# Attention of one batch woven with the projections of the next on TensorE, with 64-row score tiles and feed-forward weights streamed in pieces

## What is computed

```python
x = x + tanh(g_xattn) * attn(layernorm(x), ctx)       # ctx: 32 x 750 x 384
x = x + tanh(g_ffn)   * ffn(layernorm(x))
# attn: q = x @ Wq.T ; k, v = split(y @ Wkv.T); 16 heads of 32
attn = where(pad_mask[:, None, :, None], q @ k.T * d**-0.5, -1e9)
attn = softmax(attn, axis=-1); out = attn @ v
# ffn: bitlinear(2048) -> gelu -> bitlinear(512)
# bitlinear: weights to -1, 0, 1 by their mean size, rows of x to 255 steps
```

## Time and profile before

| | |
|---|---|
| median of 3 runs | 2122.66 us (2121.89 to 2125.13) |
| profiled run | 2131.0 us |
| its span, first to last instruction | 2129.2 us |
| mean granted TensorE clock | 0.981 |
| PE busy | 1971.3 us, 93% |
| DVE, ACT, POOL busy | 1236.9, 1060.9, 565.8 us |
| phase A, phase B | 0 to about 1587 us, to 2129 us |

### The profile page before, as it was taken

One profiled execution on the slowest core, in us unless ns is written; L12 is line 12 of the kernel. 1 busy time (PEld: TensorE's weight loads), 2 busy tenths in 40 slices (PEclk: granted clock), 3 DMA queues, 4 the chain that ended last, 5 costly groups with the idle time before them and its releaser, 6 DMA issues. The chain is left out here.

```text
span 2129.2 us, 47929 instructions
## 1 busy us (share of the span) xinstructions
PE 1971.3 (93%) x17116; PEld 1501.0 (70%) x17173; DVE 1236.9 (58%) x2371; ACT 1060.9 (50%) x1826; POOL 565.8 (27%) x619
## 2 busy tenths in 40 slices
PE   5999999999997999999999899999977888888887
PEld 4888888788886878888888688888763444444443
DVE  5455445444443444444544244444348999999996
ACT  2444433334333433333444244333346888888887
POOL 1111111111111111111111011111106777777774
PEclk9999999999998999999999899999998999999999
DMA  6000001021001003000000200001032222222221
GB/s 256 27 26 26 26 26 30 24 78 48 28 26 48 26 6 96 32 26 26 26 26 26 79 27 26 26 26 40 15 96 70 84 89 89 89 89 86 81 84 55
DMA packets 51968, 112.19 MB, mean 53 GB/s; under 512 B 5047, under 2 KB 5047, under 8 KB 51288
## 3 DMA queue, kind: packets, MB, share of 16 engines
q1 hardware_dynamic: 51928, 111.67, 15.9%
HBM read 93.36 MB, written 29.43 MB: 58 GB/s over the span
## 5 line engine op out<-in xcount | busy, mean ns | idle before, releaser
L316 POOL TENSOR_TENSOR y_l<-y,y_h 128x750 fp32r<-128x750 f32 x96 | 172.9, 1802 | 818.5 <-ACT y_h L378 818.1
L502 DVE TENSOR_REDUCE nmax<-psum 112x1 f32<-112x750 f32 x248 | 233.0, 939 | 164.3 <-PE psum L627 161.5
L400 ACT ACTIVATE prob<-psum,nmax 112x750 f32<-112x750 f32 x248 | 219.8, 886 | 92.8 <-DVE nmax L502 88.0
L1115 PE MATMUL psum<-w_q,hq_t 128*128 128x512 bf16 x841 | 194.5, 384 | 61.9 <-DVE hq_t L1014 61.9
L627 PE MATMUL psum<-y_h,wkv_h 128*128 128x512 f32 x756 | 208.4, 357 | 42.3 <-DVE wkv_l L465 14.0
L627 PE MATMUL psum<-wkv_h,y_h 128*125 128x512 f32 x558 | 226.6, 406 | 0.0
L721 PE MATMUL psum<-ident,prob 112*125 112x112 f32 x1488 | 214.9, 281 | 9.3 <-ACT prob_t L391 6.4
L627 PE MATMUL psum<-wkv_l,y_h 128*125 128x512 f32 x558 | 220.5, 395 | 0.0
L627 PE MATMUL psum<-wkv_h,y_l 128*125 128x512 f32 x558 | 220.4, 395 | 0.0
L1086 PE MATMUL psum<-w_q,xq_t 128*128 128x512 bf16 x895 | 204.6, 382 | 2.3 <-DVE xq_t L1011 2.3
L721 PEld LDWEIGHTS psum<-ident,prob 112*125 112x125 f32 x1488 | 181.3, 188 | 35.6 <-issue 22.8
(11 more groups left out here) (122 smaller groups left out, 3651.0 us busy)
## 6 DMA issues: line engine op xcount, KB each, us to landing
y<-in_ctx_t SPq DMA_DIRECT2D x32, 1125.0 KB, 5.3
xb<-in_x SPq DMA_DIRECT2D x56, 256.0 KB, 2.7
ab<-attn_rows SPq DMA_DIRECT2D x56, 256.0 KB, 2.9
out_rows<-yo SPq DMA_DIRECT2D x56, 256.0 KB, 2.0
attn_rows<-vmean_rows SPq DMA_DIRECT2D x32, 336.0 KB
w_raw<-in_w_t SPq DMA_DIRECT2D x2, 4096.0 KB, 16.6
xa<-in_x SPq DMA_DIRECT2D x32, 112.0 KB
attn_rows<-attn SPq DMA_DIRECT2D x31, 112.0 KB
```

The lines of the kernel that those rows point to most:

```text
L316: pool.tensor_tensor(y_l[:, c, :], y[:, c, :], y_h[:, c, :].bitcast(F32), ALU.subtract).then_inc(a_yl, 1)
L400: act.activation(prob[:, i % 3, :], ps_score[i % 2][0:RP, :], ACT.Exp, bias=nmax[:, i:i + 1], accum_out=den[:, i:i + 1]).then_inc(p.exp, 1)
L502: dve.tensor_reduce(nmax[:, i:i + 1], ps_score[i % 2][0:RP, :], AX.X, ALU.max, negate=True).then_inc(p.max, 1)
L1115: mm = pe.matmul(ps_y, hq_t[:, p, 128 * c:128 * c + 128], w2_q[:, c, :], start=(c == 0), stop=(c == FC - 1))
```

## The change

It rewrites phase A. **Order:** PE runs `period(b)`, which holds the attention of batch b and the projections of batch b + 1 in one fixed sequence (`ordered`); a first `period(-1)` projects batch 0. V, `y_h`, `y_l` exist twice. K is projected in halves of 376 and 374 rows, each in one bank, in two banks that K and V share. At its top a period waits until DVE has written all 8 K halves of its batch. The last K half of the next batch stands at the period's end. **Variants:** whether batch b attends and b + 1 projects is decided at run time, so `ordered` stands in the code of a period four times (both, attention only, projection only, neither), with the code for other live blocks ahead (`rest_block`) and branches between. The loop over pairs of batches holds two periods (slots j = 0 and 1). **Scores:** a group's four heads are two tiles of 64 contraction rows, issued in turn into two pairs of banks; q_h and q_l have two blocks of columns instead of four, written by two instructions of 128 rows instead of four of 32. **Weights:** pieces of 512 KB are loaded twice (for the mean, then for rounding) and DVE writes bf16 (`w_q`) in phase A, so that L992 and L963 go. **Group ends:** the mean of v uses nine fp32r matmuls, and PE doesn't wait there for its copy. **Start:** PE reads the live flags before it projects batch 0, and the low parts of both halves of Wkv are waited for.

```diff
...
-    WP = F
...
+    WP = F // 2
+    KH = ((0, M // 2 + 1), (M // 2 + 1, M))
...
-        w_raw = sb("w_raw", [128, 2 * DC * F])
...
+        w_q = sb("w_q", [128, DC * F + FC * D], BF16)
...
+        w_part = sb("w_part", [128, WP])
...
-        y_h, y_l = sb("y_h", [128, CC, M], F32R), sb("y_l", [128, CC, M], F32R)
...
+        y_h, y_l = sb("y_h", [128, 2, CC, M], F32R), sb("y_l", [128, 2, CC, M], F32R)
...
-        v = sb("v", [MC, MJ, D])
+        v = sb("v", [MC, 2, MJ, D])
...
-        ps_score = [banks[:, 2 * BANK * i:2 * BANK * i + M] for i in range(2)]
-        ps_v = [psum[0:MC, 4 + i, :] for i in range(2)]
-        ps_pt = [psum[0:MC, 4 + i, 0:MH * RP] for i in range(2)]
+        ps_score = [banks[:, 2 * BANK * e:2 * BANK * e + M] for e in range(2)]
+        ps_pt = [[psum[0:MC, 2 * e + hf, 0:MH * RP] for hf in range(2)] for e in range(2)]
+        ps_proj = [psum[:, 4 + i, :] for i in range(2)]
+        ps_xt = psum[:, 4, 0:DC * R]
+        ps_q = psum[:, 5, 0:NG * R].rearrange("p (g n) -> p g n", g=NG)
...
-        ps_xt = psum[:, 7, 0:DC * R]
-        ps_q = psum[:, 7, DC * R:DC * R + NG * R].rearrange("p (g n) -> p g n", g=NG)
...
+        k_bank = {(0, 0): 0, (0, 1): 0, (1, 0): 0, (1, 1): 0, (2, 0): 1, (2, 1): 1, (3, 0): 0, (3, 1): 1}
+        v_bank = (1, 1, 1, 1, 0, 0)
...
-        def batches(eng, batch, after_group):
+        def batches(eng, period, after_group):
...
             with eng.Fori(0, NQ - 1) as q:
-                with eng.Fori(0, QTR) as t:
-                    batch(eng.snap(q * QTR + t), True, q, t)
+                with eng.Fori(0, QTR // 2) as t:
+                    for j in range(2):
+                        period(eng.snap(q * QTR + 2 * t + j), j, q, t)
                 after_group(q)
-            with eng.Fori((NQ - 1) * QTR, B - 1) as b:
-                batch(b, True, NQ - 1, None)
-            after_group(NQ - 1)
-            batch(B - 1, False, NQ - 1, None)
+            q = NQ - 1
+            with eng.Fori(0, QTR // 2 - 1) as t:
+                for j in range(2):
+                    period(eng.snap(q * QTR + 2 * t + j), j, q, t)
+            after_group(q)
+            for j in range(2):
+                period(B - 2 + j, j, q, QTR // 2 - 1)
+
...
+                def weights(b, q, t, j):
...
+                    sp.wait_ge(a_wuse, b + ONE)
+                    sp.sem_inc(met_sp, 1)
+                    if isinstance(q, int):
...
+                        return
+                    with sp.If(q == 1):
+                        sp.dma_start(by_cols, w2_in()).then_inc(a_w, 16)
+                    with sp.Else():
+                        sp.dma_start(w_part[:], w1_in()).then_inc(a_w, 16)
...
-                def scores(p, n0, i):
...
-                def project_k(g, chunks):
+                def scores(p, slot, g):
+                    for n, (qs, ks) in enumerate(((q_h, k_h), (q_h, k_l), (q_l, k_h))):
+                        for s0, s1 in SEGS:
+                            for e in range(2):
+                                r = slice(PW * e, PW * e + PW)
+                                mm = pe.matmul(ps_score[e][0:RP, s0:s1], qs[r, slot, g, :, :].rearrange("p e r -> p (e r)"),
+                                               ks[r, g, s0:s1], start=(n == 0), stop=(n == 2))
+                                if n == 2 and s1 == M:
+                                    mm.then_inc(p.s, 1)
+
+                def k_half(slot, g, hf, chunks=range(CC)):
+                    s0, s1 = KH[hf]
+                    w = slice(128 * g, 128 * g + 128)
+                    out_ = ps_proj[k_bank[g, hf]][:, 0:s1 - s0]
                     for c in chunks:
-                        w = slice(128 * g, 128 * g + 128)
-                        mm = split_product(ps_score[g % 2], wkv_h[:, c, w], wkv_l[:, c, w],
-                                           y_h[:, c, :], y_l[:, c, :], c == 0, c == CC - 1, SEGS)
-                    return mm
-
-                def project_v(nl, j):
-                    if j == 0:
-                        pe.wait_ge(last.pa, NP * nl + ONE)
-                    elif j == 1:
-                        pe.wait_ge(last.pd, NP * nl + ONE)
-                    elif j % 2:
-                        pe.wait_ge(a_vd, MH * nl + j // 2 + ONE)
-                    else:
-                        pe.wait_ge(a_va, MH * nl + j // 2 + ONE)
+                        for n, (ws, ys) in enumerate(((wkv_h, y_h), (wkv_h, y_l), (wkv_l, y_h))):
+                            mm = pe.matmul(out_, ws[:, c, w], ys[:, slot, c, s0:s1],
+                                           start=(c == 0 and n == 0), stop=(c == CC - 1 and n == 2))
+                    if c == CC - 1:
+                        mm.then_inc(a_k, 1)
+
+                def v_chunk(slot, i):
+                    mcols = slice(MC * i, MC * i + MC)
+                    out_ = ps_proj[v_bank[i]][0:MC]
                     for c in range(CC):
...
+                        for n, (ys, ws) in enumerate(((y_h, wkv_h), (y_h, wkv_l), (y_l, wkv_h))):
+                            mm = pe.matmul(out_, ys[:, slot, c, mcols], ws[:, c, D:],
+                                           start=(c == 0 and n == 0), stop=(c == CC - 1 and n == 2))
                     mm.then_inc(a_v, 1)
...
+                def ordered(b, j, q, na, attends, projects):
+                    n0 = pe.snap(na * NP + ONE) if attends else None
+                    m = na + 1 if attends else na
+                    here, ahead = j, (j + 1) % 2
+                    pe.wait_ge(a_kl, 2 * NG * m + ONE)
+                    if projects:
+                        pe.wait_ge(a_yl, CC * (b + 2) + ONE)
+                    if attends:
+                        pe.wait_ge(last.ql, 2 * (na + 1) + ONE)
+                        pe.wait_ge(last.pa, n0)
+                        pe.wait_ge(last.pd, n0)
+                        scores(last, here, 0)
+                    if projects:
+                        turn(last, b + 1)
+                        v_chunk(ahead, 0)
+                    else:
+                        pe.sem_inc(last.xt, 1)
+                    live_pe.next(b)
+                    if projects:
+                        pe.wait_ge(last.xe, m + 1 + ONE)
+                        k_half(ahead, 0, 0)
+                    if attends:
+                        turn_prob(last, n0, 0, 0)
+                        turn_prob(last, n0, 0, 1)
+                    if projects:
+                        pe.wait_ge(a_va, MH * m + 1 + ONE)
+                        v_chunk(ahead, 1)
+                    if attends:
+                        pe.wait_ge(last.pa, n0 + 2)
+                        pe.wait_ge(last.pd, n0 + 2)
+                        scores(last, here, 1)
+                        pe.wait_ge(last.on, na + ONE)
+                        pe.wait_ge(a_vme, q + ONE)
+                        if not isinstance(q, int):
+                            pe.wait_ge(a_wmean, q + ONE)
+                        else:
+                            pe.wait_ge(a_wmean, NQ - 1 + ONE)
+                        pe.wait_ge(a_va, MH * (na + 1) + ONE)
...
+                    if projects:
+                        pe.wait_ge(a_kl, 2 * NG * m + 1 + ONE)
+                        k_half(ahead, 0, 1)
+                        pe.wait_ge(a_vd, MH * m + 1 + ONE)
+                        v_chunk(ahead, 2)
+                    if attends:
+                        turn_prob(last, n0, 1, 0)
+                        turn_prob(last, n0, 1, 1)
+                    if projects:
+                        pe.wait_ge(a_kl, 2 * NG * m + 2 + ONE)
...
+                    if attends:
+                        turn_out(last, na, 2)
+                        weighted(last, n0, here, 3)
+                    if projects:
+                        pe.wait_ge(a_kl, 2 * NG * m + 6 + ONE)
+                        k_half(ahead, 3, 1, (0, 1))
+                    if attends:
+                        turn_out(last, na, 3)
+                        sums(last)
+                    if projects:
+                        k_half(ahead, 3, 1, (2,))
+                    pe.sem_inc(a_yfree, 1)
+
+                def rest_block(n, na, here, other):
...
+                    for g in range(NG):
+                        pe.wait_ge(rest.pa, n0 + 2 * g)
...
+                        scores(rest, other, g)
+                        for e in range(2):
+                            turn_prob(rest, n0, g, e)
+                        weighted(rest, n0, here, g)
...
+                def period(b, j, q, t):
+                    kd, kn, nl, nr = live_pe.now()
+                    projects = projects_ahead(b)
...
                     with pe.If(kd > 0):
...
                         with pe.If(kd > 1):
...
                             with pe.Fori(0, RB) as k:
...
+                                rest_block(pe.snap(nr + k), nl, j, (j + 1) % 2)
...
+                            pe.sem_inc(met_pe, 1)
+                        if projects:
+                            with pe.If(kn > 0):
```

(33 more changed lines are left out.)

828 lines of the change are left out of this document (453 added, 375 removed).

## The result

| | before | changed |
|---|---|---|
| median | 2123.89 us (4 runs) | 2550.57 us (4 runs, 2545.63 to 2552.87) |
| ratio | | 1.2005, 95% interval 1.1981 to 1.2029 |
| profiled span | 2129.2 us | 2543.8 us |
| granted clock | 0.981 | 0.879 |

The account below looks back on a forecast made before the run. PE's own work was taken to bound the kernel. Profiled 2131 us, less 141 of gains, plus 348 (336 jump stalls + 48 half clock - 36 covered bubble), gave 2338; median 2330 us, range 2090 to 2490.

Parts of the forecast that it names:

- PE bounds, and the period's work: Phase A: PE's work sets the 47.96 us interval; overlapping score tiles and fewer waits bring a full period to 43.3 us.
- Loops that don't fit: PE's loop grows from 1,826 to 5,334 instructions and no longer stays on chip, so jumps wait in every pass.
- The price of a jump: Jumps between periods: long 4.0 us, short 2.0; stalls of 8.4 and 14.4 us in turn, together 336.
- the short one: PE's jump over the projection-only variant, 346 instructions, maybe fetched ahead: 2.0 us, half of a long one.
- What hides: Matmuls still in PE's queue at a period's end cover about 1.6 us of the jumps.
- Half clock and base: PE restarts at half clock after each stall, 1.6 us, 30 times, 48 us, on a period of 43.3.
- DVE has spare time: In phase A DVE uses 23 of 48 us; weight rounding is a piece in each period as before.
- Group ends, 3.3 us: Nine fp32r matmuls (2.1 us) and 1.2 of waits leave 3.3 us over a plain interval, 13.2 for four.
- L992: Its 4.43 us go from the start of phase B, which brings nothing; were it on the path, 4.4.
- The rival with no jumps, 1982: No wait at jumps, so the gains stand: 1982 us, 1960 to 2020; chance 0.16.
- the 141 us: Gain over the whole run without the jump term: 1587 to 1446, putting the profiled run of 2131 at 1990.

Follow-up runs that it names:

- best: one_way with weight rounding behind the fourth V copy, group-end stores spread over periods, and last K halves ahead of the last V chunk: 2031.90 us, ratio to before 0.9559.
- one_way: The changed kernel with one sequence per period on every engine, without variants or code for other live blocks: 2175.6 us, ratio to before 1.0231.
- b_pad100: The kernel before with 100 never-run instructions at the end of PE's part of a live batch, jumped over each time: 2217.9 us (one run).

## Why the prediction was right and wrong

- **PE bounds, and the period's work.** Right. 47.96 became 43.6 where nothing stalls it (best), against 43.3 forecast. The 64-row tiles overlap as the column tiles do: 1.1 us a group, where 1.03 were assumed and 2.06 was the price before.
- **Loops that don't fit.** Right, and the step that decided the sign. The earlier trace rows held: what three first passes cost, every pass costs once the loop is too long. The bound itself, taken as somewhere between 1,826 and 5,334, is 1,675 to 1,803 for a straight loop.
- **The price of a jump.** This is the term that failed. The sum took 4.0 us for a long jump, 2.0 for the short one and nothing for the way between them. Measured in the two plain steps shown, the short one (L990, 346 instructions) costs 4.8; the long ones cost 3.7 and 4.4 from slot 0 to 1, and 3.5, 3.0, 4.7 and, for the jump back, 6.4 from slot 1 to 0; the way between them takes 1.6 and 1.7. What hides, 1.6 us, was right. So PE's idle time was 12.8 and 17.7 us, not 8.4 and 14.4. Of the 4.4 us more in the first, 2.8 are the short jump and 1.6 the way; of the 3.3 in the second, 2.4 are the jump back and 1.7 the way, and the others came out 0.8 cheaper. Over the whole run the idle time with "issue" as its end at a period's start is 438 us (405.4 at the scores, 23.9 at the group ends, 8.6 at the dead batch) and not 336: 102 of the 207 us missed. "Maybe fetched ahead" was a guess with no row under it, and so was the half price; the price doesn't follow the length of the jump.
- **Half clock and base.** 45.8 and 46.3 us of PE busy time an interval against 43.3 + 1.6: 1.1 us too little, 34 in all. The row at 794.76 showed half clock for 3.35 us; behind these longer stalls it lasts to 249.4 and 191.4, 4.7 and 5.8 us from the first scores.
- **"DVE has spare time".** Wrong in kind. 23 of 48 us says nothing of when. The rounding stands in front of q_l, which PE needs: 47 us in one_way. In the changed kernel the later intervals are 60 to 61 and 65 us, some 1.5 us longer than the first.
- **Group ends, 3.3 us.** Wrong: 6 to 8 us in the changed kernel, 12 to 20 in one_way. PE's own steps were costed, SP's queue, which the working named with the loads but not with the stores, was not. That the stores are the cause was tried on one_way alone.
- **L992.** Right: phase B takes 544 us from the last PE work of phase A, as before (2543.8 - 1999.8, 2129.2 - 1585.5).
- **The rival with no jumps, 1982.** Also too good: one_way shows that the other new waits would have left little. Of the 141 us, 95 were there only after three more edits. Of the 207 us by which the profiled run was missed, the jumps' idle time and the half clock make 136, the rounding and the group ends some 30; the rest lies at the start (first scores at 62.8, not 60.5) and around the dead batch, and was not taken apart.

## What to carry to other kernels

Count PE's instructions in the loop, dead branches included, before writing a variant into it. Here a straight loop of 1,675 stayed and one of 1,803 was fetched anew in every pass (143 pieces against 52), and with skipped code inside a loop of 1,846 could wait; each longer jump then cost 2 to 6.5 us in every pass, and one over 346 instructions as much as one over 695. Choose the variant once outside the loop. When work is woven, read for each wait what stands queued behind it on its engine; a busy share of half does not say that the engine is free when it is needed.

## What the runs showed of the hardware that was not expected

- A straight loop waits at its jump back from 1,803 instructions on (3.3 us at least). At 1,675 it waits in 3 passes of the whole run, two of them at the loop over groups. In the kernel before, whose loops have some 750 instructions skipped inside, the second copy waits at 1,846 and not at 1,796; the first doesn't at 1,896, but its loop over groups does at 1,926 and not at 1,876. Moving loops by 140 or 236 instructions changed nothing. Why the first copy fits more stays open.
- Of the branches only PE's wait: in b_pad100, L209 takes 4361 ns at the median on PE and 45 to 63 ns at the median on the other engines. No run here shows how long their loops may be.
- Idle time with "issue" as its end needs no jump: in the second copy of b_pad100 PE also stood so among the scores, for 2.2 to 2.7 us. That it waited for instructions there is likely and not shown.
- Two 64-row tiles overlap in part even where six matmuls of one stand ahead of six of the other (1.7 us a group, against 1.1 in turns and 2.06 for full tiles).
- A DVE step of 128 x 1024 values (maximum and minimum, float32) takes 0.69 us alone and 2.2 to 2.7 us in each pass in which it stood beside POOL's subtraction; that POOL is the cause is read from the times, and from the move that ended it, not from a run without POOL.
